# A decoder layer on one core: three steps of the attention stage written in another order

## What is computed

```python
x = _layernorm(x + _L0_attn_ref(x, w_qkv, b_qkv, w_proj, b_proj))          # causal, 16 heads of 16
x = _layernorm(x + _L0_xattn_ref(x, ctx, ctx, w_q, w_k, w_v, w_o))         # 16 heads of 64, 77 keys
x = _layernorm(x + _L0_ffn_ref(x, k0, k1, k2, s0, s1, s2))                 # weights of +1 and -1

# causal self-attention
scores = jnp.einsum('bhqd,bhkd->bhqk', q, k) * scale
scores = jnp.where(causal, scores, -jnp.inf)
attn = jax.nn.softmax(scores, axis=-1)
out = jnp.einsum('bhqk,bhkd->bhqd', attn, v)
```

## Time and profile before

| what | us |
|---|---|
| median of three runs | 2189.83 |
| lowest and highest run | 2187.28, 2194.01 |
| the profiled execution | 2191.86 |
| its span | 2190.1 |
| TensorE busy in the span | 2112.3 (96%) |
| VectorE busy | 1501.4 (69%) |
| ScalarE busy | 1134.8 (52%) |
| GpSimd busy | 669.8 (31%) |

### The profile page before, as it was taken

The page is one execution under the profiler, slowest core; times in us unless marked ns, Lnnn a source line. Parts: engine busy times, 40 slices in busy tenths (PEclk is TensorE's granted clock), DMA queues, the critical chain, the costliest instruction groups (busy, mean ns, idle before and its releaser), DMA issues.

```text
span 2190.1 us, 54589 instructions
## 1 busy us (share of the span) xinstructions
PE 2112.3 (96%) x18572; PEld 1868.8 (85%) x18572; DVE 1501.4 (69%) x4647; ACT 1134.8 (52%) x2571; POOL 669.8 (31%) x751
## 2 busy tenths in 40 slices
PE   8998689999999999999999999999999999999998
PEld 7887578888888888888888888888888888888887
DVE  5553467777777777777777777777777777777764
ACT  5554445555555545555555555445555555555553
POOL 2000223333333333233333333333333333333331
PEclk9999899999999999999999999999999999999999
DMA  8997532233333333322333333333223332333310
GB/s 270 310 295 208 133 72 63 63 72 73 56 65 77 77 77 77 72 66 62 70 73 63 58 77 77 77 77 75 65 63 67 73 67 54 77 77 77 77 44 10
DMA packets 180580, 196.57 MB, mean 90 GB/s; under 512 B 50131, under 2 KB 135155, under 8 KB 180467
## 3 DMA queue, kind: packets, MB, share of 16 engines
q1 hardware_dynamic: 180532, 195.94, 38.6%
HBM read 69.37 MB, written 58.87 MB: 59 GB/s over the span
## 4 chain that ended last, share of the span: by engine, by line
PE 82%; ACT 6%; issue 4%; DVE 4%; DMA 2%; SPq 1%; POOL 1%; ACTq 0%; POOLq 0%; DVEq 0%
PE ps L1202 13%; PE ps L1385 11%; PE ps L1243 9%; PE ps L1244 9%; PE ps L1351 5%; PE ps L1279 5%; PE ps L1211 4%; PE ps L1226 3%; PE ps L1294 3%; PE ps L1268 3%; PE ps L1369 3%; PE ps L1183 2%; ACT probs L651 2%; PE ps L1152 2%; PE ps L1254 2%
## 5 line engine op out<-in xcount | busy, mean ns | idle before, releaser
L1243 PE MATMUL ps<-r_h,w 128*128 128x256 f16 x2048 | 461.9, 273 | 1.6 <-DVE r_l L843 1.6
L1244 PE MATMUL ps<-r_l,w 128*128 128x256 f16 x2048 | 460.6, 273 | 0.0
L857 DVE CUSTOM_DVE_ANT_0 junk<-ps,causal 128x128 bf16<-128x128 f32 (+1 forms) x1024 | 331.2, 356 | 127.1 <-PE ps L1268 116.2
L503 POOL TENSOR_SCALAR_AFFINE_SELECT probs<-probs 128x512 f32<-128x512 f32 x256 | 163.3, 638 | 465.0 <-ACT probs L651 460.7
L526 POOL TENSOR_TENSOR rstd<-var_eps,minus_half 128x2 f32<-128x2 f32 x96 | 66.9, 696 | 670.5 <-DVE var_eps L832 670.5
L626 ACT ACTIVATE p2r<-ps,low 128x77 f32<-128x77 f32 x1024 | 243.2, 340 | 43.6 <-DVE low L896 42.9
L517 POOL TENSOR_TENSOR p<-p2r,inv 128x308 f32<-128x308 f32 x256 | 201.2, 787 | 196.6 <-DVE inv L907 192.8
L1385 PE MATMUL ps<-vo_h,p2t 128*128 128x256 f32 (+1 forms) x1280 | 239.4, 290 | 8.0 <-DVE p2t L914 8.0
L1243 PEld LDWEIGHTS ps<-r_h,w 128*128 128x128 f16 x2048 | 200.2, 98 | 35.7 <-issue 9.5
L589 ACT ACTIVATE r_h<-ps 128x512 f16<-128x512 f32 x256 | 148.8, 597 | 154.0 <-PE ps L1244 139.2
L843 DVE SCALAR_TENSOR_TENSOR r_l<-ps,r_h 128x512 f16<-128x512 f32 x256 | 172.9, 686 | 75.3 <-ACT r_h L589 75.2
(11 more groups left out here) (145 smaller groups left out, 4736.2 us busy)
## 6 DMA issues: line engine op xcount, KB each, us to landing
vo_scratch<-vo_out SPq DMA_DIRECT2D x80, 448.0 KB, 5.3
vo<-vo_scratch SPq DMA_DIRECT2D x64, 512.0 KB
q_st<-p2t SPq DMA_DIRECT2D x192, 128.0 KB
k_bd<-p2t SPq DMA_DIRECT2D x192, 128.0 KB, 6.4
q<-q SPq DMA_DIRECT2D x128, 128.0 KB, 2.1
k_bd<-k_scratch SPq DMA_DIRECT2D x64, 154.0 KB, 3.5
x_in<-in_x SPq DMA_DIRECT2D x32, 256.0 KB, 2.7
out<-y SPq DMA_DIRECT2D x32, 256.0 KB, 6.4
```

The lines of the kernel that those rows point to most:

```text
L857: dve.tensor_tensor_reduce(out=junk[:, e, b * P:b * P + width], in0=ps[:, bank + b, e * width:(e + 1) * width], in1=causal[:, (1 - b) * P: ...
L1243: pe.matmul(dst, w1[:, kk, m * P:(m + 1) * P], r0_h[:, kk, :], start=kk == 0, stop=False)
L1244: last = pe.matmul(dst, w1[:, kk, m * P:(m + 1) * P], r0_l[:, kk, :], start=False, stop=kk == KF - 1)
```

## The change

On ScalarE the exponential of pair 4 is put in front of `self_output(i, 0)`. On TensorE `scores_by_key(i, 4)` is put in front of `queries_keys(i + 1, 0)` and with it in front of the first two `values`, and `filler0(1)` is put in front of `scores_by_key(i, 6)`. Both hold for all 32 passes, as far as a pass has the step. Every wait stays with its step. VectorE, GpSimd and SyncE keep their programs.

```diff
@@ ScalarE, attention
                     transposed_x2(f)
                 if more:
                     queries_keys(i + 1, 0)
+                self_probs(i, 4)
                 self_output(i, 0)
-                self_probs(i, 4)
                 self_probs(i, 5)
                 self_probs(i, 6)
@@ TensorE, attention
                     transposed_x2(f)
+                scores_by_key(i, 4)
                 if more:
                     queries_keys(i + 1, 0)
                 values(i, 0)
                 values(i, 1)
-                scores_by_key(i, 4)
                 scores_by_key(i, 5)
                 filler0(0)
+                filler0(1)
                 scores_by_key(i, 6)
-                filler0(1)
                 if more:
                     queries_keys(i + 1, 1)
                 scores_by_key(i, 7)
```

## The result

| | before | after |
|---|---|---|
| median of four runs, us | 2190.89 | 2224.15 |
| lowest and highest run | 2187.28, 2194.01 | 2222.58, 2225.68 |
| the profiled execution | 2191.86 | 2223.83 |
| its span | 2190.1 | 2222.1 |

The ratio of the times is 1.015, with a 95% interval of 1.0137 to 1.0163: the change makes the kernel slower by 1.5%, or 33 us. Predicted were 2229 us, 5 us more.

The account below looks back on a forecast made before the run. TensorE's order was taken to bound the kernel. Thirty passes at 1.1 us (33), pass 0 (4.5) and the last pass (1.9) make 39 us: median 2229 us, between 2220 and 2240; 2216 to 2248 including the last rival.

Parts of the forecast that it names:

- The wait: TensorE, scores of pair 4: they wait for the two small maxima DMAs and start 2.48 us after the first issue.
- The 2.7 us: Alternative issue-to-scores time: about 2.0 us fixed DMA cost applied to the second copy; final time some 7 us longer.
- What comes back: TensorE, first to second queries and keys: 0.73 us of the 1.62 us delay returns, leaving 0.89 us a pass.
- The gap in front of the last `values`: TensorE's 0.55 us wait for GpSimd: stays, since its chain moves with the late second queries and keys.
- The rival by which it swallows part of it: The 0.55 us gap before the last `values` does not move, so a pass costs 0.55 us: 2213 us, chance 0.08.
- The VectorE term: Late output copy delays reciprocal and L843, so `layer0` of m = 4 waits: 0.2 us a pass, between 0 and 0.4.
- The ends: Pass 0 and the last pass, outside the thirty loop passes: 4.5 us and 1.9 us longer.
- What the change removes: TensorE's wait of the scores of pair 6 for the exponential of pair 4: 0.32 us gone in each pass.
- Not slower: Rival: the maxima are there in time, each pass gains 0.5 us if at once: 2175 us, chance 0.04.
- The clock: Rival: a 1.4 us gap each pass drops TensorE to 1.2 GHz, 5.1 us a fall: 2382 us, chance 0.06.
- The output copy's lateness goes further: Rival: its DMAs meet the next queries' copies, or VectorE holds more `layer0` parts, another 0.5 us a pass: 2244 us, chance 0.08.

Follow-up runs that it names:

- `layer0` part alone: Kernel before with only `filler0(1)`, `layer0` of m = 1, put in front of `scores_by_key(i, 6)` on TensorE: 2180.84 us, ratio 0.9942.

## Why the prediction was right

The mechanism is the one told. The wait list has the new row L1279 on `q_st<-neg_max`, 33 times; moving the scores one step back removes it and the loss with it (2183.74 us), and lengthening it by copies lengthens the pass. The size was a little too high: 0.85 us a pass lies just under the prediction's lower bound of 0.9. (Its upper bound of 1.4 is not what its terms give, which is 0.9 + 0.4 = 1.3.) Point by point:

- **The wait.** Predicted were 2.48 us from the first issue to the scores, from the last pass; measured 2.59. The figure of the last pass was the right one to take (the last pass of after has 2.49), and the 4.36 us of the earlier trace rows belonged to pass 0 alone. The 2.7 us, an estimate from the Trainium skill's page for another path than SyncE's, is as near to 2.59 as 2.48 is, but the final time by it, some 7 us more, would have been further off.
- **What comes back.** Predicted 0.73, measured 1.73 - 0.94 = 0.79 up to the second queries and keys, and another 0.10 from there to the last `values`, where I had said that nothing shrinks: the first two matmuls of the second queries and keys take 0.40 us instead of 0.49. Together that is 0.89. So the pass is 0.85 us longer where I had 0.89: the start was 0.11 us later than told and the return 0.16 us larger. That the two nearly cancel is luck.
- **The gap in front of the last `values`** stayed (18.6 us in 32 waits; 18.2 before), so it moved with the delay. The rival by which it swallows part of it (2213 us) falls.
- **The VectorE term** was mis-sized: predicted 0.2 us a pass, measured 0. The output copy and the reciprocal came as late as told (1.71 and 1.70, for 1.77), but the lateness shrank on its way: 1.53 at the second L871 pair and 1.12 at L843. I had taken off 0.31 us, the idle time in front of L843. The start of L843 came 0.41 nearer to L871, since rows that follow without idle time overlap by 0.1 (0.78 us from start to start for 0.87 of length), and the second L871 pair came 0.17 nearer to the reciprocal (2.14 us behind it, 2.31 before). L843 then ends just when `layer0` of m = 4 is due. The wait list shows 6.8 us in 31 waits of the weight load for it, but in before 5.9 us in 30 stood there as issue time, so the name changed and the time hardly did; from the last `values` to `layer0` it is 0.79 us in both. This term, 30 x 0.2 = 6 us, is about all by which the forecast is too high.
- **The ends.** Predicted 4.5 + 1.9 = 6.4 us for pass 0 and the last pass. Measured 3.7 and 2.2. Pass 1 came out at 1.8, where I had 1.1 as for the others, and the first issue 0.9 us earlier, of which I had nothing. Together 6.8 us, where my terms for the same places make 6.4 + 1.1 = 7.5. (Part of this is the clock: around the issue of pass 1, at 304.76, after has 17.0 us at a granted clock of 0.50, from 296.4 to 313.4, where before has 10.2.)
- **What the change removes** was right: 0.32 us predicted, 0.35 measured for the `layer0` part alone. But the credit belongs to that part. The exchange on ScalarE, which I had not costed by itself, is worth 0.1 us in this order of TensorE, and costs 0.85 in the old. Of the 1.71 us by which the output copy is late the exchange makes only 0.05: the copy stands 6.23 us behind the issue without it and 6.28 with it, and 4.57 before.
- **Not slower** (2175 us) needed a landing within 1.6 us. Even with one copy it was 1.86, and the pass 0.11 us longer than before.
- **The clock** did not fall in the loop of after. It was nearer than the 0.06 suggests: with 0.62 us more of idle time it fell in 3 of 29 passes, and with the scores alone it fell in one, behind a landing that was late. Two waits of 2.06 us in the version with ScalarE's old order left it up, so the length of the gap alone does not decide. But a fall in the loop cost 1.55 to 1.60 us, not the 5.1 of the prediction, since it lasted 3.4 us and not 10.2; thirty of them would have made some 47 us and not 153.
- **The output copy's lateness goes further** (2244 us): it did not in after, but in the exchange-alone version it did, for 0.81 us of wait on L843, 0.4 of it from a mechanism that I had not thought of, the stretched product beside the select. In after the product starts at 1234.26 and ends at 1234.68, and the select of pair 7 starts at 1234.76. Only products that began behind a select's start were stretched, so what keeps after from paying this too is 0.5 us.

The parts alone are worth +1.42, -0.35 and +0.85 us a pass, 1.92 in sum; together they cost 0.85. Built up in a row they are 61.57 us with the scores, 61.09 with the `layer0` part, and 61.00 with the exchange: +1.42, -0.48 and -0.09. What differs is above all the exchange. In the old order it makes the output copy 1.42 us late, since the exponential has to wait for its scores, and `layer0` of m = 4 is due at its old time. With the scores in front the exponential has its input early and delays the copy by 0.05 us only. The copy is late there because of the scores, and this lateness is hidden, since `layer0` is due 0.85 us later too.

## What to carry to other kernels

A step whose operand comes by a small DMA must stay behind enough other work, counted from the last issue to the use; take the price from the pass in which the trace shows this wait uncovered, the first or the last one of a loop, since the covered passes don't show it. A late start on a side engine costs only what is left when its idle time on the way is used up, so follow each step and subtract each gap. And measure the parts of a reordering one by one and together: here one part alone was a gain of 0.6%, and one cost 1.2% alone and nothing in company, since the other part had given it its input early.

## What the runs showed of the hardware

- VectorE's product of two SBUF operands (128 x 256, L887) took 0.42 us, and 0.85 us when it began 0.06 us behind the start of GpSimd's select of 128 x 512 (0.64 us); it ended 0.28 us behind the select's end. A zeroing of 32 x 128 beside it did nothing to it (0.43). A select that began 0.01 us behind the product's start took 0.91 us, and the product 0.42.
- Small copies, SBUF to SBUF, issued by SyncE: a single one of 8 KB was usable by TensorE 1.86 us after its issue began, the last of two of 4 KB 2.59 us after the first issue. With one or two spare copies of 4 KB to device memory ahead of these two it was 3.21 and 3.84 us.
- Idle gaps of 1.36 us a pass left TensorE at 2.4 GHz; with 1.98 us the granted clock fell to 1.2 GHz in 3 of 29 passes, with 2.61 us in 26 of 29, at a price of 1.55 to 1.60 us a fall. Single gaps of 2.06 us (two) left it up, one of 2.18 us brought it down.
